# DLRM tower with a compressed interaction network: products written with even embedding dims first, halves added on VectorE, sums over 16 rows

## What is computed

```python
# e: (512, 40, 32), one gathered table row per sample and field
h = e
for i, (W, bias) in enumerate(params):            # three layers
    x = einsum('bhd,bmd->bhmd', h, e).reshape(B, -1, D)
    y = relu(einsum('oi,bid->bod', W, x) + bias[None, :, None])
    if i != n_layers - 1:
        h, direct = split(y, 2, axis=1)           # 100 maps go on, 100 go out
    else:
        direct = y
    outs.append(direct)
z = concatenate(outs, axis=1).sum(-1)             # (512, 400), the sum is over the 32 dims
# then a three-layer perceptron on [z, dense_ctx]
```

## Time and profile before

| | |
|---|---|
| median of 3 runs | 2907.57 us (2905.47 to 2908.14) |
| the profiled execution | 2907.22 us |
| its span | 2905.5 us |
| TensorE busy | 2830.5 us (97%) |
| VectorE busy | 2607.7 us (90%) |
| ScalarE busy | 1502.0 us (52%) |
| GpSimd busy | 688.1 us (24%) |
| mean granted TensorE clock | 0.993 of full speed |

### The profile page before, as it was taken

The page is one execution under the profiler, slowest core; times in us unless marked ns, Lnnn a source line. Parts: engine busy times, 40 slices in busy tenths (PEclk is TensorE's granted clock), DMA queues, the critical chain, the costliest instruction groups (busy, mean ns, idle before and its releaser), DMA issues.

```text
span 2905.5 us, 54782 instructions
## 1 busy us (share of the span) xinstructions
PE 2830.5 (97%) x19516; PEld 2811.0 (97%) x19516; DVE 2607.7 (90%) x1751; ACT 1502.0 (52%) x1880; POOL 688.1 (24%) x669
## 2 busy tenths in 40 slices
PE   2899999999999999999999999999999999999998
PEld 2899999999999999999999999999999999999996
DVE  4899999999999999999999999999999999999993
ACT  2555555555555555555555555555555555555552
POOL 2122222222222222222222222222222222222000
PEclk8999999999999999999999999999999999999999
DMA  6434333334333334333334334334333334334320
GB/s 158 101 67 100 86 74 97 86 74 98 87 74 96 87 74 99 87 74 97 87 75 98 86 74 97 87 75 96 89 73 96 88 75 99 87 75 94 95 57 21
DMA packets 280089, 249.92 MB, mean 86 GB/s; under 512 B 27803, under 2 KB 278602, under 8 KB 279965
## 3 DMA queue, kind: packets, MB, share of 16 engines
q1 hardware_dynamic: 211192, 196.57, 23.8%
q0 software_dynamic: 59744, 45.90, 11.0%
q10 hardware_dynamic: 9129, 7.13, 1.0%
HBM read 140.44 MB, written 4.20 MB: 50 GB/s over the span
## 4 chain that ended last, share of the span: by engine, by line
PE 96%; DMA 1%; SPq 1%; DVE 1%; issue 1%; ACT 0%; POOL 0%; DVEq 0%; ACTq 0%; POOLq 0%
PE acc L717 62%; PE acc L719 29%; PE z_ps L734 3%; PE hid_ps L730 1%; SPq L349 1%; PE acc L777 0%; DMA x_pairs<-x_rows 0%; DVE product L660 0%; DMA raw_weights<-in_w 0%; DVE tails L665 0%; PE hid_ps L800 0%; SPq L321 0%; DMA hid_rep<-hid 0%; POOL gathered L410 0%; DMA starts_sb<-in_table_starts 0%
## 5 line engine op out<-in xcount | busy, mean ns | idle before, releaser
L717 PE MATMUL acc<-weights,heads 126*128 126x400 f32 (+1 forms) x9088 | 2707.9, 365 | 62.3 <-DVE tails L665 62.3
L719 PE MATMUL acc<-weights,tails 126*128 126x200 f32 (+1 forms) x9088 | 2324.3, 256 | 0.0
L484 ACT ACTIVATE heads<-product 126x1024 fp32r<-126x1024 f32 (+2 forms) x1152 | 1203.9, 1048 | 1149.9 <-PE acc L719 749.5
L717 PEld LDWEIGHTS acc<-weights,heads 126*128 126x128 f32 (+1 forms) x9088 | 1717.0, 189 | 63.8 <-issue 46.6
L719 PEld LDWEIGHTS acc<-weights,tails 126*128 126x128 f32 (+1 forms) x9088 | 1744.7, 192 | 0.0
L660 DVE TENSOR_TENSOR product<-hid_rep,x_rep 126x2048 f32<-126x2048 f32 x512 | 1172.5, 2290 | 214.8 <-PE acc L719 175.5
L665 DVE TENSOR_TENSOR tails<-product,heads 126x1024 fp32r<-126x1024 f32 (+2 forms) x1152 | 1338.4, 1203 | 3.4 <-ACT heads L484 3.4
L418 POOL TENSOR_TENSOR wait_taker<-wait_taker 1x1 f32<-1x1 f32 x192 | 106.8, 556 | 2069.0 <-ACT acc_copy L490 2067.3
L410 POOL DMA_INDIRECT gathered<-in_table,rows_now x150 | 316.5, 2110 | 45.7 <-issue 45.7
L495 ACT ACTIVATE y_relu<-acc_copy 128x400 f32<-128x400 f32 x192 | 102.4, 533 | 192.8 <-DMA acc_copy<-acc_copy 192.8
L419 POOL DMA_DIRECT2D acc_copy<-acc_copy x192 | 175.8, 916 | 1.1 <-issue 0.6
(11 more groups left out here) (27 smaller groups left out, 106.4 us busy)
## 6 DMA issues: line engine op xcount, KB each, us to landing
x_rep<-x_rows SPq DMA_DIRECT2D x512, 120.0 KB
hid_rep<-hid SPq DMA_DIRECT2D x512, 120.0 KB
x_pairs<-x_rows SPq DMA_DIRECT2D x192, 280.0 KB
acc_copy<-acc_copy POOLq DMA_DIRECT2D x192, 200.0 KB
hid_rep<-hid SPq DMA_DIRECT2D x512, 5.0 KB
x_pairs<-x_rows SPq DMA_DIRECT2D x64, 120.0 KB
raw_weights<-in_w ACTq DMA_DIRECT2D x12, 492.2 KB
x_rep<-x_rows SPq DMA_DIRECT2D x128, 20.0 KB
```

Of the source, the lines that this page charges most:

```text
L484: act.activation(heads[0:rows, ring % HEADS_RING, 0:tiles, :], product[0:rows, ring % PRODUCT_RING, 0:tiles, :], ACT.Copy).then_inc(heads_ ...
L717: nc.tensor.matmul(acc[:, at.parity, c, 0:2 * LAYER], heads[0:rows, ring % HEADS_RING, k, cols], w, start=(q == 0 and k == 0), stop=False)
L719: last = nc.tensor.matmul(acc[:, at.parity, c, LAYER:2 * LAYER], tails[0:rows, ring % PRODUCT_RING, k, cols], w[:, 0:LAYER], start=False, ...
```

## The change

The products of a block are written in another column order: column h*128 + s*16 + m holds sample s and dim 2m + h. So the first column group holds the even dims of all eight samples, the second the odd dims. The two inputs of the multiplication are read in their old order, so successive elements go out in turn to the two halves of the tile, 128 elements (512 bytes) apart. TensorE's transposes write `hid_ps` with a step of two columns, which puts the dims back into their old order. After the relu VectorE adds the two column groups of `y_relu` into `y_fold` (`fold`, 100 elements a partition in layers 0 and 1, 200 in layer 2), and the sum over the dims goes over runs of 16 rows against `sum16`, [128, 8]: one matmul in layers 0 and 1, two in layer 2. TensorE waits for the fold before these matmuls, and VectorE waits for the relu before the fold, at fixed places of its order.

```diff
@@ dims of a column group
+        def dims(columns, c):
+            return columns[:, c * 128:(c + 1) * 128]
...
@@ make_products
-                dve.tensor_tensor(out, first, second, ALU.mult).then_inc(products_made, 2)
+                tiles = out.shape[1] if layer == 0 else 2 * GROUP
+                if layer > 0:
+                    out = out.rearrange("p a b c -> p (a b) c")
+                out = out.rearrange("p t (h m) -> p t m h", h=CG)
+                halved = "p t (m h) -> p t m h" if layer == 0 else "p a b (m h) -> p a b m h"
+                if layer > 0:
+                    out = out.rearrange("p (a b) m h -> p a b m h", a=2)
+                dve.tensor_tensor(out, first.rearrange(halved, h=CG), second.rearrange(halved, h=CG),
+                                  ALU.mult).then_inc(products_made, 2)
...
+            def fold(layer, at, b):
+                first = HALF if layer < 2 else 0
+                dve.wait_ge(y_relued, at.slot + 1)
+                above_zero(dve, y_turned, at.slot)
+                dve.tensor_tensor(y_fold[:, first:LAYER], y_relu[:, 0, first:LAYER], y_relu[:, 1, first:LAYER],
+                                  ALU.add).then_inc(y_folded, 1)
+
-            def make_previous_tails(g, ring):
+            def make_previous_tails(g, ring, between=None):
                 layer, q = previous[0]
-                for n in (2, 1):
-                    make_tails(layer, q + 2 - n, g - n, (ring - n) % RING)
+                make_tails(layer, q, g - 2, (ring - 2) % RING)
+                if between:
+                    fold(*between)
+                make_tails(layer, q + 1, g - 1, (ring - 1) % RING)
                 previous[0] = None
@@ step on VectorE
                         make_products(layer, at, q, i - layer, parity)
+                        between = None
+                        if first and layer == first[0] and q == 4 and before and before[0] > 0:
+                            between = before
+                        if second and layer == second[0] and q == 6:
+                            between = first
                         if previous[0]:
-                            make_previous_tails(at.group + q, at.ring + q)
+                            make_previous_tails(at.group + q, at.ring + q, between)
+                            if l0 and first and layer == first[0] and q == 6:
+                                fold(*l0)
...
@@ turn on TensorE
-                        nc.tensor.transpose(hid_ps[0:HALF, layer, c * 128:(c + 1) * 128], y_relu[:, c, 0:HALF], ident[:, :])
+                        nc.tensor.transpose(hid_ps[0:HALF, layer, c:COLS:CG], y_relu[:, c, 0:HALF],
+                                            ident[:, :])
+                pe.wait_ge(y_folded, at.slot + 1)
                 for n, first in enumerate((HALF,) if layer < 2 else (0, HALF)):
-                    for c in range(CG):
-                        at_col = n * BLOCK + c * (BLOCK // CG)
-                        last = nc.tensor.matmul(z_ps[0:HALF, at.parity, at_col:at_col + BLOCK // CG],
-                                                y_relu[:, c, first:first + HALF], sum32[:, :], start=True, stop=True)
+                    last = nc.tensor.matmul(z_ps[0:HALF, at.parity, n * BLOCK:(n + 1) * BLOCK],
+                                            y_fold[:, first:first + HALF], sum16[:, :], start=True, stop=True)
```

More of the change, by code:

```diff
@@ L36 @@
 CG = COLS // 128
+DIM_HALF = DIM // CG
 DUO = 2 * BLOCK
@@ L76, in cin_kernel @@
 def cin_kernel(nc, ids, table_starts, table, w0a, w0b, w1, w2, dense_t, wt1z, wt1d, wt2, wt3, bt1, bt2,
-               ident_in, sum32_in, out):
+               ident_in, sum16_in, out):
     duos = ids.shape[1]
@@ L135, in cin_kernel @@
         y_relu = sb("y_relu", [128, CG, LAYER])
+        y_fold = sb("y_fold", [128, LAYER])
         hid = [sb(f"hid{n}", [HALF, COLS]) for n in (1, 2)]
@@ L144, in cin_kernel @@
         ident = sb("ident", [128, 128])
[L145 removed]
+        sum16 = sb("sum16", [128, BLOCK])
         dense_sb = sb("dense_sb", [DENSE, batch])
@@ L190, in cin_kernel @@
         y_relued = sem("y_relued")
+        y_folded = sem("y_folded")
         y_turned = sem("y_turned")
@@ L312, in _ @@
                 sp.dma_start(swapped(n), w0b[:, t:t + k, :]).then_inc(swapped_loaded[n], 16)
-            for dst, src in ((ident[:, :], ident_in), (sum32[:, :], sum32_in), (dense_sb[:, :], dense_t),
+            for dst, src in ((ident[:, :], ident_in), (sum16[:, :], sum16_in), (dense_sb[:, :], dense_t),
                              (wt1d_sb[:, :], wt1d), (wt3_sb[:, :], wt3), (bt1_sb[:, :], bt1), (bt2_sb[:, :], bt2)):
@@ L670, in _ @@
             previous = [None]
-            def make_previous_tails(g, ring):
+            def fold(layer, at, b):
[5 more added lines that the diff above has]
+            def make_previous_tails(g, ring, between=None):
                 layer, q = previous[0]
-                for n in (2, 1):
-                    make_tails(layer, q + 2 - n, g - n, (ring - n) % RING)
+                make_tails(layer, q, g - 2, (ring - 2) % RING)
+                if between:
+                    fold(*between)
+                make_tails(layer, q + 1, g - 1, (ring - 1) % RING)
                 previous[0] = None
             def step(i, odd):
+                before, l0, l1, l2 = slots_of(i, odd)
+                first, second = (l1, l2) if l1 else (l2, None)
                 for layer in range(3):
@@ L692, in step @@
                             make_previous_tails(at.group + 2, at.ring + 2)
+                        if before and before[0] == 0 and layer == 0:
+                            fold(*before)
                         if odd is None:
@@ L698, in _ @@
             make_previous_tails(total_groups, total_groups)
+            fold(2, place(2, blocks - 1), blocks - 1)
         @block.tensor
@@ L715, in accumulate @@
                     for c in range(CG):
-                        cols = slice(c * 128, (c + 1) * 128)
-                        nc.tensor.matmul(acc[:, at.parity, c, 0:2 * LAYER], heads[0:rows, ring % HEADS_RING, k, cols], w,
+                        nc.tensor.matmul(acc[:, at.parity, c, 0:2 * LAYER], dims(heads[0:rows, ring % HEADS_RING, k, :], c), w,
                                          start=(q == 0 and k == 0), stop=False)
-                        last = nc.tensor.matmul(acc[:, at.parity, c, LAYER:2 * LAYER], tails[0:rows, ring % PRODUCT_RING, k, cols],
+                        last = nc.tensor.matmul(acc[:, at.parity, c, LAYER:2 * LAYER], dims(tails[0:rows, ring % PRODUCT_RING, k, :], c),
                                                 w[:, 0:LAYER], start=False, stop=(q == last_q and k == tiles - 1))
@@ L863, in build @@
                args["w2"], args["dense_t"], args["wt1z"], args["wt1d"], args["wt2"], args["wt3"], args["bt1"],
-               args["bt2"], args["ident"], args["sum32"], out)
+               args["bt2"], args["ident"], args["sum16"], out)
 def kernel(**inputs):
```

2 lines of the change are left out of this document (1 added, 1 removed).

## The result

The changed kernel takes 3702.9 us (median, 3688.6 to 3717.7) against 2906.5 us before, a ratio of 1.274 with a 95% interval of 1.270 to 1.279. The profiled execution took 3697.9 us, 791 us more than the 2907.2 before. The forecast was slower, 3500 us, with a range from 2860 to 3850. The ratios of all kernels here leave out runs that took over 1.5% more than the fastest of the same kernel; only two runs of `hop_only` did.

The account below looks back on a forecast made before the run. TensorE was taken as the bound at 43.54 us a pass, VectorE close behind. VectorE's pass would become 39.8 + 0.7 + 12.6 = 53.1 us, +9.6 us, 605 us over 63 passes: 3512, put at 3500 us, range 2860 to 3850.

Parts of the forecast that it names:

- TensorE's share: Half of the sum matmuls leave TensorE: 0.61 us a pass, 39 us over 64 blocks, leaving TensorE 42.9 us a pass.
- The folds: VectorE's added folds of the column groups, two of 100 elements and one of 200: 0.7 us a pass, inside its spare time.
- Hardly waiting: Expected sign on VectorE: 192 folds of 0.25 and 0.36 us that hardly wait.
- The transposes with a step of two: TensorE's transposes writing with a step of two: taken as costing nothing, at most 0.44 us a pass.
- the other end: Upper bound for TensorE's transposes with a step of two: twice the time, 0.44 us a pass, 28 us in all.
- The hopping write: VectorE's products written in turns to two places 512 bytes apart: two thirds of a cycle more an element, 12.6 us a pass.
- The waits at the folds: VectorE's folds waiting for relus and TensorE for the work behind: all three waits cost nothing at the products' old speed.
- the free write: Rival 1: VectorE's hopping write costs nothing and TensorE stays the bound, 2868 us, or 2896 with dear transposes; chance 0.25.
- the one over a cycle: Rival 2: VectorE's hopping write costs more than a cycle extra an element; at 1.4 cycles 4390 us; chance 0.06.
- the cancelling of loss and gain: Rival 4: the write costs about a tenth of a cycle and waits at the turns take back 39 us, 2907; chance 0.02.
- The clock: Rival 3: TensorE's clock falls because it idles a fifth of the time, mattering under 0.81; at 0.5, 5580 us; chance 0.02.
- The signs: Expected profile marks: products some 3.7 us, VectorE nearly always busy, folds hardly waiting, L734 at its old mean, ScalarE waiting little for TensorE.

Follow-up runs that it names:

- hop_only: The kernel before with only the new write: products written with even dims first, no folds; ratio 1.290, some 3749 us.
- no_hop: The changed kernel, but VectorE writes the products contiguously in the old column order; 2868.1 us, ratio 0.987.
- patterns: No tower: VectorE multiplies 2048 elements a partition in 14 write and read patterns, ScalarE copies 1024 in four; contiguous 2292 ns, hop of 512 bytes 3717 ns.
- runs16: The whole change with dims 0 to 15 in the first column group and 16 to 31 in the second, so VectorE writes runs of 16; 2873.2 us, ratio 0.988.
- shared_port: No tower: GpSimd does eight one-element adds alone, then beside contiguous, then hopping VectorE multiplications; 183 ns alone, 2137 ns and 6308 ns on average beside them.

## Why the prediction was right, and where it was short

*TensorE's share:* right. 0.61 us a pass and 39 us in all; `no_hop` gave 2868.1 against 2868, with 42.85 us a pass against 42.9.

*The folds:* right in size. They last 0.26 us for 100 elements and 0.37 for 200, and 0.18 and 0.27 us from start to start, so 0.63 us a pass against 0.7. In `no_hop` they lie beside other work. "Hardly waiting" failed.

*The transposes with a step of two:* right at nothing. The sentence of the Trainium skill cited for the other end (PSUM — Partial Sum Buffer, its table of properties) is not borne out here for fp32 transposes, 273 ns against 273.

*The hopping write:* the deciding term, right in kind, small in size. I chose two thirds of a cycle, and no row stood behind that choice, so that it came close is luck; alone the write does cost two thirds, (3717 - 2292) / 2048 = 0.70 ns of the 1.047 ns of a cycle. In the kernel the durations give (3910 - 2290) / 2048 = 0.79 ns, 0.76 of a cycle. Longer products also overlap more with what follows, so from start to start a product grew from 2.21 to 1502.96 - 1499.21 = 3.75 us and that of layer 0 from 1.94 to 1551.03 - 1547.75 = 3.28: 8 x 1.54 + 1.34 = 13.7 us a pass in place of 12.6. The pass came to 54.1 us where the sum said 53.1, and 63 x 1.0, some 60 us of the miss, are this term. That VectorE's pass would be the bound, and TensorE's 42.9 us inside, held.

*The waits at the folds:* this is the step that failed. That "all three waits cost nothing at the old speed of the products" was worked out at a speed that the next paragraph gave up. At the new one VectorE waits 125 us there. I had the slack between each relu and its fold (1.2, 0.07 and -0.3 us) but took the relus' own times as fixed, where they hang on GpSimd, whose add already took 556 ns in place of the 183 it takes alone. 3512 + 60 + 125 = 3697 us, against the 3697.9 of the profiled execution; as said above, the ends of the kernel make that fit closer than its terms are.

*Rivals:* the free write is out (`patterns`), the one over a cycle too, and with 3703 us so is the cancelling of loss and gain. The clock fell to 0.96, far above the 0.81 at which it would have mattered.

*The signs:* two more than the quiet folds did not come. ScalarE still waits 754 us for TensorE before its heads (749.5 before), and the matmuls of the sums average 235 ns, not the old 218. VectorE's products and tails are the largest named part of the chain that ended last, with 24% and 8% of the span; GpSimd's add has 7%, and 43% are time in which nothing was waited for that the profile shows.

## What to carry to other kernels

Work out the spare time of the second busiest engine before giving it a new layout to write: here it was 3.7 us in 43.5, and the write alone took 13.7. Writing fp32 elements one by one in turns to two places costs VectorE 62% more time alone and 71% in the kernel, runs of two on an even word cost nothing, so look for the split that keeps a run (and fits the dimensions of an instruction) before putting it on either engine: `runs16` is 34 us faster than the kernel before, of the 39 us. And when an engine becomes the bound, price the waits again at its new pace, on every queue whose small instructions have to slip in between its large ones.

## What the runs showed of the hardware

- VectorE alone, fp32, 2048 elements: 2292 to 2294 ns for contiguous writes, runs of 2, 4 and 16 and a steady step of two, 3717 for single elements in turn at 512 bytes or more, 3788 at 32 bytes, 2864 for runs of two from an odd word. Reading one input in turns costs 2328.
- Single elements in turn in the kernel: 3910 ns, and near 3.72 us where TensorE stands still.
- ScalarE, 1024 elements: 1056, 1973 with the write in turns, 1283 with the read in turns.
- An add of one element on GpSimd takes 183 ns alone. Beside back-to-back VectorE instructions with two inputs in SBUF it takes one of them (2.12 or 3.49 us), or stays out for several: 14.59 us in `hop_only`, 39.16 us in `shared_port`, until VectorE stopped.
- A weight load with a step of two columns takes 195 ns against 189 (heads), 198 against 192 (tails).
